# Adding the attention branch to its residual on GpSimd instead of on TensorE, in a fused decoder layer

## The reference, cut to what matters

```
q, k, v, window gates = projections of x          # silu, per-head layer norm of q and k
attn[.., w]  = softmax over the 17 neighbours     # 16 heads of 16, gated window
out          = sum over w of attn[.., w] * v[l + w - 8]
y            = silu(out @ Wout)
x            = layernorm(x + y)                   # over the 256 channels, no gain
```

## Time and profile before

| | |
|---|---|
| median of 3 runs | 1187.74 us |
| the profiled execution, its own time | 1187.74 us |
| its span, first to last instruction | 1185.5 us |
| busy in the span: TensorE matmul | 960.9 us (81%) |
| busy: VectorE | 825.9 us (70%) |
| busy: GpSimd | 712.9 us (60%) |
| busy: ScalarE | 461.7 us (39%) |
| mean granted TensorE clock | 0.927 |

### The profile page before, as it was taken

The page is one execution under the profiler, slowest core; times in us unless marked ns, Lnnn a source line. Parts: engine busy times, 40 slices in busy tenths (PEclk is TensorE's granted clock), DMA queues, the critical chain, the costliest instruction groups (busy, mean ns, idle before and its releaser), DMA issues.

```text
span 1185.5 us, 25126 instructions
## 1 busy us (share of the span) xinstructions
PE 960.9 (81%) x8135; PEld 774.8 (65%) x8136; DVE 825.9 (70%) x1264; ACT 461.7 (39%) x1055; POOL 712.9 (60%) x464
## 2 busy tenths in 40 slices
PE   7983089998989989678788249999999999999940
PEld 4541088888879979656566237777777777777720
DVE  4899999999999998138888764444444444444425
ACT  3676224444444444325656223222222222222215
POOL 3575599999999999200000055666666666666522
PEclk9998589999999999879999569999999999999985
DMA  3262012112211221478674402222222222222236
GB/s 102 72 120 54 22 41 67 53 58 67 66 56 54 67 66 45 168 256 273 193 236 160 164 28 37 47 41 47 42 46 41 45 44 44 44 45 44 27 80 226
DMA packets 70136, 100.46 MB, mean 85 GB/s; under 512 B 9312, under 2 KB 51872, under 8 KB 69152
## 3 DMA queue, kind: packets, MB, share of 16 engines
q1 hardware_dynamic: 52816, 76.86, 20.8%
q0 software_dynamic: 16128, 18.93, 10.1%
q10 hardware_dynamic: 1152, 4.19, 0.9%
HBM read 73.96 MB, written 26.38 MB: 85 GB/s over the span
## 4 chain that ended last, share of the span: by engine, by line
PE 44%; DVE 28%; issue 15%; DMA 5%; POOL 3%; ACT 3%; DVEq 0%; SPq 0%; ACTq 0%; POOLq 0%
PE psum L757 16%; DVE mid L1392 11%; PE psum L765 10%; PE psum L767 5%; PE psum L616 3%; PE psum L685 2%; DMA sum_dram<-arena,mid 2%; DVE psum L1399 2%; PE psum L596 2%; DVE arena L1529 1%; PE psum L749 1%; PE psum L659 1%; ACT arena L1082 1%; PE psum L599 1%; DMA out<-arena 1%
## 5 line engine op out<-in xcount | busy, mean ns | idle before, releaser
L616 PE MATMUL psum<-consts,mid 128*128 128x128 f32 x2176 | 255.5, 279 | 58.4 <-POOL mid L1155 58.4
L616 PEld LDWEIGHTS psum<-consts,mid 128*128 128x128 f32 x2176 | 251.9, 195 | 66.6 <-issue 48.2
L757 PE MATMUL psum<-arena 128*128 128x128 f16 x3456 | 291.2, 221 | 4.6 <-issue 2.7
L757 PEld LDWEIGHTS psum<-arena 128*128 x3456 | 243.4, 98 | 76.2 <-issue 9.5
L1155 POOL TENSOR_TENSOR mid<-arena 128x2304 f32<-128x2304 f32 (+1 forms) x62 | 251.1, 4072 | 10.0 <-POOL arena L1146 7.0
L765 PE MATMUL psum<-arena 128*128 x576 | 218.1, 380 | 5.3 <-DVE arena L1681 1.2
L1233 POOL DMA_INDIRECT sum_dram<-arena,mid x72 | 142.0, 1972 | 46.5 <-issue 24.3
L1690 DVE SCALAR_TENSOR_TENSOR arena<-psum,arena 128x256 f32<-128x256 f32 x72 | 34.8, 484 | 189.8 <-ACT arena L1054 121.4
L767 PE MATMUL psum<-arena 128*128 x576 | 157.0, 273 | 0.0
L1054 ACT ACTIVATE arena<-psum,arena 128x256 f32<-128x256 f32 x72 | 34.1, 473 | 301.5 <-PE psum L767 301.5
L1392 DVE TENSOR_TENSOR mid<-psum,arena 128x4352 f32<-128x4352 f32 x32 | 149.9, 4683 | 0.6 <-issue 0.4
(11 more groups left out here) (194 smaller groups left out, 1443.3 us busy)
## 6 DMA issues: line engine op xcount, KB each, us to landing
arena<-w_t SPq DMA_DIRECT2D x64, 256.0 KB, 2.8
arena<-w_t SPq DMA_DIRECT2D x16, 1024.0 KB, 10.4
arena<-x SPq DMA_DIRECT2D x32, 128.0 KB, 2.1
arena<-x_dram SPq DMA_DIRECT2D x8, 512.0 KB, 5.5
arena<-ctx_t SPq DMA_DIRECT2D x8, 512.0 KB, 6.4
arena<-ctx SPq DMA_DIRECT2D x8, 512.0 KB, 6.9
x_dram<-mid SPq DMA_DIRECT2D x8, 512.0 KB, 3.3
arena<-sum_dram SPq DMA_DIRECT2D x8, 512.0 KB, 4.9
```

The costliest lines, as they stand in the source:

```text
L616: last = nc.tensor.matmul(psum[:, u, c * P:(c + 1) * P], products[half][:, w, c * P:(c + 1) * P], ident, start=(a + w == 0 and c == 0), st ...
L757: last = nc.tensor.matmul(dst, block_of(w, e, 0, c * F + j * P, P), x[:, u, c * P:(c + 1) * P], start=(k == 0 and c == 0), stop=(k == 2 an ...
```

## The change

TensorE no longer adds x to silu(y). `add_x` and its PSUM area are gone. GpSimd's `silu_y` becomes `silu_add_x`: the product that ends the silu, a wait for its own completion, a wait for the load of x, and an addition in place into `x_res`. ScalarE's `keep` reads `x_res` in SBUF instead of PSUM. SyncE now waits for `keep` before it loads the next x into the buffer (`res_kept` instead of `res_summed`). At the end, `keep(29)` moves ahead of `take_mean(28)` and `mixed_out(30)`.

```diff
@@ sync, load_x_res
                 if past(t, 2):
-                    sp.wait_ge(res_summed, t - 1)
+                    sp.wait_ge(res_kept, t - 1)
@@ tensor, mix
                 if past(t, 2):
                     pe.wait_ge(y_parts, t - 1)
-                    pe.wait_ge(res_kept, t - 1)
...
                 last.then_inc(y_done, 1)
-                if past(t, 1):
-                    add_x(t - 1, 1 - u, i if u else i - 1)
-
-            def add_x(t, u, i):
-
-                pe.wait_ge(x_res_loaded[u], 16 * i + 16)
-                pe.wait_ge(silu_y_made, t + 1)
-                nc.tensor.matmul(res_psum[:, u, :], ident, x_res[:, u, :], start=True, stop=False, skip_group_check=True)
-                nc.tensor.matmul(res_psum[:, u, :], ident, tanh_y[:, u, :], start=False, stop=True,
-                                 skip_group_check=True).then_inc(res_summed, 1)
...
-            add_x(CHUNK - 1, 1, CHUNK // 2 - 1)
@@ scalar, keep and the end
-                nc.scalar.activation(row(q_all, t), res_psum[:, u:u + 1, :], ACT.Copy,
+                nc.scalar.activation(row(q_all, t), x_res[:, u:u + 1, :], ACT.Copy,
...
+            keep(CHUNK - 3, 1)
             take_mean(CHUNK - 4)
             mixed_out(CHUNK - 2, 0)
-            keep(CHUNK - 3, 1)
             take_spread(CHUNK - 4)
@@ gpsimd
-            def silu_y(t, u):
+            def silu_add_x(t, u, i):
                 pool.wait_ge(y_parts, t + 1)
-                nc.gpsimd.tensor_tensor(tanh_y[:, u, :], tanh_y[:, u, :], y_sb[:, u, :], ALU.mult).then_inc(silu_y_made, 1)
+                done(nc.gpsimd.tensor_tensor(tanh_y[:, u, :], tanh_y[:, u, :], y_sb[:, u, :], ALU.mult), silu_y_made, t + 1)
+                pool.wait_ge(x_res_loaded[u], 16 * i + 16)
+                nc.gpsimd.tensor_tensor(x_res[:, u, :], x_res[:, u, :], tanh_y[:, u, :], ALU.add).then_inc(res_summed, 1)
...
-                    silu_y(t - 2, u)
+                    silu_add_x(t - 2, u, i - 1)
```

More of the change, by code:

```diff
@@ L315, in decoder_layer @@
         squares_beside = psum[:, 7, 0:E]
-        res_psum = psum[:, 4:6, E:2 * E]
         head_sum = psum[:, 4, 0:4 * H].rearrange("p (u x) -> p u x", u=2)
@@ L1196, in _ @@
             norm_part(3)
-            silu_y(CHUNK - 2, 0)
-            silu_y(CHUNK - 1, 1)
+            silu_add_x(CHUNK - 2, 0, CHUNK // 2 - 1)
+            silu_add_x(CHUNK - 1, 1, CHUNK // 2 - 1)
             norm_part(4)
```

## The result

The changed kernel takes 1205.2 us (median of 4 runs, 1202.16 to 1206.12), the kernel before 1186.74 us in the same comparison: a ratio of 1.0153, 95% interval 1.0128 to 1.0178. The forecast was 1205.5 us. The profiled execution took 1203.33 us with a span of 1201.5 us, 16.0 us longer than that of before. Lines have moved. On GpSimd L1155 is now the subtraction of the peak, L1133 the probabilities, L1142 the products with v, L1147 the silu product, L1149 the new addition. On TensorE L615 is the group of products, L623 y = mixed @ Wout. On ScalarE L868 is the exponential, L848 copies the transposed sum out, L887 squares the weights, L893 is `keep`. L1414 is VectorE's sum of the exponentials, L546 the first load of the cross attention.

The account below looks back on a forecast made before the run. The prediction took VectorE as setting the pace before and GpSimd as the bound after. From 1187.74 us it added 20.8 for the stage's delay at step 31 and subtracted 3.0 at the end: 1205.5 us, range 1200 to 1211.

Parts of the forecast that it names:

- The bound: Window steps: the addition, 0.98 us, exceeds GpSimd's spare 0.41 us; GpSimd becomes the bound with steps of 11.25 us.
- The first rival: Window steps: VectorE stays the bound, loops cost nothing, only the end gets shorter, 1184.3 us; chance 0.05.
- One sign: Steady steps: GpSimd busy for 97 us or more of 100 if the forecast is right.
- The gap: GpSimd's self-wait before the addition: 0.25 us in the loops, making 0.98 us a step, bounds 0.80 and 1.03.
- `norm_part` in full: GpSimd in the loops: `norm_part`, formerly paid back from slack, counts in full, 2.19 us three times.
- VectorE: Window steps: VectorE waits for the exponential in every step but adds no wait of its own, no second chain.
- SyncE's wait costs nothing: Weight loads in the steps: they go out some 0.5 us later behind `keep`, costed at nothing.
- The clock costs nothing in the loops: TensorE in the loops: a step with a clock fall takes 11.1 us, still under 11.25, costed at nothing.
- The end, minus 3.0 us: From step 31 to the end of the window stage: 3.0 to 3.9 us shorter, taken as 3.0.
- the last hop: End of the stage, last addition to `keep`: 1.6 us over GpSimd instead of 2.01 over TensorE, 0.4 earlier.
- The large term: End of the stage, TensorE from `y` to the next product group: 1.6 to 2.5 us earlier without the two pairs.

Follow-up runs that it names:

- Experiment 1: Changed kernel without GpSimd's addition and its self-wait, x left out of the residual: 1188.17 us, ratio 1.0022 to the kernel before.
- experiment 2: Changed kernel with a second, unused addition of the same shape on GpSimd: 1223.24 us, ratio 1.0331 to the kernel before.
- experiment 3: Changed kernel with the addition one step later on GpSimd, between the probabilities and the first product with v: 1191.74 us, ratio 1.0054 to the kernel before.
- experiment 4: Kernel before with one line of the change, SyncE waiting for `keep` instead of for the sum: 1187.01 us, ratio 1.001.
- experiment 5: Pair of idle matmul operations added on TensorE, in the changed kernel (1203.68 us, ratio 1.0145) and in the kernel of Experiment 1 (1185.51 us, ratio 1.0).
- experiment 6: Kernel before with GpSimd adding x only for steps 29 to 31, `keep(29)` moved ahead and SyncE waiting for `keep`: 1186.08 us, ratio 0.9995.
- experiment 8: ScalarE's six normalisations moved behind `mixed_out(30)`, on top of experiment 6 (1182.31 us, ratio 0.9971) and in the kernel before (1184.09 us, ratio 0.9985).

## Why the prediction was right

The time, 1205.5 us against 1205.2, is better than its terms deserve. Part of it is luck in the value that it starts from: the sum adds 17.8 us to 1187.74, but the kernel before took 1186.74 us beside the changed one and 1185.84 (35 runs) later. The loss itself is 18.5 us by the medians and 18.1 by the ratio, and from 1185.84 the same sum would have given 1203.6. By its own steps:

- *The bound.* Right. GpSimd had 0.41 us a step to spare and got 0.81 to 0.94 us of work: 0.73 for the addition and a gap of 0.08 or 0.19. Experiment 1 takes the work away and most of the 18 us with it, experiment 2 adds nearly as much again and the loss doubles. The first rival, VectorE as the bound, is out. One sign did not come: GpSimd was to be busy for 97 us or more of 100 and was for 95.89. That sign did not fit the prediction's own sum, in which 0.55 us of a step of 11.25 are gaps.
- *The gap.* Mis-sized: I took 0.25 us in the loops and 0.98 us a step; start to start it was 0.81 us in one step of the loop body and 0.92 to 0.94 in the other (334.47 to 335.28, 323.24 to 324.18), so a step was 11.16 us and not 11.25. I explained 0.22 us of the gap at L1146 by register work for a count and an address. With another instruction in the gap nothing of it remains (experiment 3). Against that, step 6 started 0.9 us later than in my sum (199.84, not 198.94), as TensorE's first group let GpSimd go on 0.8 us later than in the trace before (157.61 against 156.79). With the next point, step 31 came at 485.88, not 486.7.
- *`norm_part` in full.* Right, and a little low: the three steps with it are 2.31, 2.28 and 2.59 us longer than the 11.10 us of such a step, 7.2 in all where the sum has 6.6. In experiment 3 it is 7.2 us again, with steps as short as VectorE's.
- *VectorE.* Right that there is no second chain in the loops (experiment 2), wrong in the picture: L1414 waited for the exponential in 12 of 23 steps, 16.3 us in all, and not in every one. Where it did not wait it ran ahead.
- *SyncE's wait costs nothing.* Right, experiment 4.
- *The clock costs nothing in the loops.* Right for this kernel: seven L615 groups were slow in the trace after, the mean clock there 0.95, and filling the pauses (0.99) left the 25 steps at 286 us. But only because GpSimd is slower still. Without the addition such pauses cost some 2 us in the steps (272.1 us from step 6 to step 31, 270.2 with the pairs) and 2.7 us by the medians (experiments 1 and 5): when GpSimd catches up with steps of 10.3 us, a TensorE step with a slow group, 11.1 us or more, is the longer one. My sum for the first rival, 1184.3 us, had left that out: with VectorE as the bound experiment 1 is 2.6 us slower than the kernel before (1.3 to 4.0 by its ratio), where I had a gain of 3.4.
- *The end, minus 3.0 us.* The trace shows 3.17 us, and this is the step that was right for the wrong reason. `mixed_out(30)` came only 0.2 us earlier and not 1.0 (501.86, 15.98 us behind step 31, against 16.21), as the squares came 11.3 us behind step 31 (497.18) and not 10.4: ScalarE waited 4.67 us for their load. From L623 to the next L615 it took 0.97 us where it had taken 3.45, 2.5 earlier and not 1.6, and the last hop (513.67 to 515.23) gave 0.45. The large term is the clock's. I compared the pairs at half clock with nothing, as if they were gone and the slow time with them. In experiment 6 L617 moved into the slow time instead and the gain was gone. The trace of after shows 3.17 us since its clock stayed up after a pause of 2.58 us and that of before fell after 2.13. Like with like, the end costs 29.35 us after against 30.37 in experiment 4, both at full clock, and 32.22 in experiment 6 against 32.52 before, both after a fall. So about 1.0 and 0.3 us are the change's own, from one trace each; ends after a fall scatter more than that (31.30 in experiment 3, with the same work at the end as in 6). That fits the medians, which are 18.5 us apart, while the two profiled executions are 15.6 apart.

Granted clock as this case shows it: in the loops of the changed kernel it fell after pauses of 1.56 and 1.74 us and stayed up after others of 1.57 and 1.74, at the same place in the step; in experiment 3 it fell after two of 1.19. After each of the nine pauses of 3.0 to 3.4 us before a product group, in four kernels, that group was slow. The Trainium skill (TensorE: Matmul & The Clock Gate, Part 1) says that the turning points vary from run to run, because what watches the activity runs freely. The ends of these traces agree that it varies, and no run here shows the reason: nine of them have a pause of 2.1 to 2.9 us there, and the clock fell in five, after 2.13 us (before) and 2.69 (experiment 6) for two, and not in four, after 2.27 (experiment 4) and 2.58 (after) for two. What stays open is how often the end falls in each kernel: every trace is one execution.

## What to carry to other kernels

Before work is moved to an engine, take that engine's spare time per step from steps in which it waited for nobody, not from its busy share: here 0.41 us against an addition of 0.87, and at 95.9% busy it was the bound, since its other idle time was for its own results. Where an in-order engine must wait for its own result, put an independent instruction of the same engine there: that took some 12 of the 18 us back. And relieving TensorE was worth nothing, or less, where it waited for others: look at what its clock does with the longer pause, and cost what follows at both clocks.

## What the runs showed that was not expected

- GpSimd's gap for its own result varied by the place in an unrolled loop body, 0.08 and 0.19 us behind L1147, 0.28 to 0.30 behind L1133, and was zero with another instruction in between.
- With two idle matmul operations a step added, the median of a kernel fell by 2.7 us (1188.17 to 1185.51 us), with the mean granted clock at 0.99 instead of 0.96 in the steps.
- The version of experiment 8, with the change kept to the last three steps and ScalarE's normalisations moved, takes 1182.31 us: 0.29% under the kernel before, 1.9% under the changed one (1182.31 / 1205.2, from two comparisons).
